# First attention of a four-layer gated network on one NeuronCore: softmax weights divided before they are transposed, the value product taken with V stationary, and the context read already transposed

## What is computed

```python
# first attention; "x" here is the context, "latents" the normalised running x
xn = layer_norm(x, gamma_x, beta_x)             # ctx_1024
ln = layer_norm(latents, gamma_l, beta_l)
q = (ln @ Wq).reshape(b, m, 8, 64) * 64 ** -0.5
k_x, v_x = xn @ Wkv;  k_l, v_l = ln @ Wkv
k_x = rope_rotate_k(k_x)
k = concat([k_x, k_l]);  v = concat([v_x, v_l])  # 64 + 64 keys
attn = softmax(einsum('bhid,bhjd->bhij', q, k))
out = einsum('bhij,bhjd->bhid', attn, v) @ Wo
# x = x + tanh(g_xattn[0]) * out
```

## Time and profile before

| | us |
|---|---|
| median of 3 runs (lowest to highest) | 2242.03 (2236.01 to 2242.62) |
| the profiled execution | 2245.91 |
| its span, first to last instruction | 2244.1 |
| mean granted TensorE clock of the span | 0.944 |

### The profile page before, as it was taken

The page is one execution under the profiler, slowest core; times in us unless marked ns, Lnnn a source line. Parts: engine busy times, 40 slices in busy tenths (PEclk is TensorE's granted clock), DMA queues, the critical chain, the costliest instruction groups (busy, mean ns, idle before and its releaser), DMA issues. The chain is left out here.

```text
span 2244.1 us, 48290 instructions
## 1 busy us (share of the span) xinstructions
PE 1965.8 (88%) x18173; PEld 1522.7 (68%) x18173; DVE 1700.4 (76%) x4753; ACT 1192.8 (53%) x2324; POOL 262.5 (12%) x553
## 2 busy tenths in 40 slices
PE   3999999999986998999989886999999986499808
PEld 3788888888876897777757665577777765244307
DVE  2787887878866887999967786766666668787894
ACT  1555555555543215888866553544454445316844
POOL 0011111011101101111111142000000022200000
PEclk9999999999997998999989998999999998699958
DMA  6222221212213551111100011222221111001462
GB/s 184 50 49 49 51 50 47 51 49 50 51 32 152 227 228 26 32 33 30 33 8 1 10 48 55 78 77 103 87 76 76 76 43 34 0 1 72 172 205 76
DMA packets 123591, 155.71 MB, mean 69 GB/s; under 512 B 47561, under 2 KB 104290, under 8 KB 119266
## 3 DMA queue, kind: packets, MB, share of 16 engines
q1 hardware_dynamic: 117368, 149.92, 20.8%
q10 hardware_dynamic: 5994, 2.70, 0.4%
HBM read 110.11 MB, written 25.69 MB: 61 GB/s over the span
## 5 line engine op out<-in xcount | busy, mean ns | idle before, releaser
L1720 DVE TENSOR_TENSOR arena<-arena 128x512 f32<-128x512 f32 (+1 forms) x256 | 170.7, 685 | 68.9 <-ACT arena L1758 64.8
L1758 ACT ACTIVATE arena<-banks,b1c 128x512 f32<-128x512 f32 x192 | 131.7, 687 | 170.4 <-PE banks L1633 170.2
L1643 PEld LDWEIGHTS banks<-w2a,arena 128*128 128x128 f32 x1024 | 124.1, 192 | 28.6 <-issue 28.6
L888 PE MATMUL banks<-we,arena 128*128 128x128 f32 x1024 | 132.9, 284 | 4.4 <-DVE arena L952 0.5
L491 PE MATMUL banks<-arena,wk 128*128 128x128 f32 x1024 | 134.5, 286 | 1.1 <-DVE arena L609 1.1
L888 PEld LDWEIGHTS banks<-we,arena 128*128 128x128 f32 x1024 | 122.5, 195 | 12.8 <-DVE arena L952 12.4
L491 PEld LDWEIGHTS banks<-arena,wk 128*128 128x128 f32 x1024 | 122.1, 196 | 12.4 <-issue 10.7
L1643 PE MATMUL banks<-w2a,arena 128*128 128x128 f32 x1024 | 124.7, 275 | 0.0
L595 DVE TENSOR_TENSOR arena<-arena,konst 128x512 f32<-128x512 f32 x64 | 44.3, 693 | 104.3 <-DMA arena<-arena 104.3
L1633 PE MATMUL banks<-arena,w1s 128*128 128x512 f32 x256 | 122.1, 611 | 0.0
L501 PE MATMUL banks<-wv,arena 128*128 128x512 f32 x256 | 120.9, 595 | 0.0
(11 more groups left out here) (271 smaller groups left out, 5091.5 us busy)
## 6 DMA issues: line engine op xcount, KB each, us to landing
arena<-coef_scratch SPq DMA_DIRECT2D x32, 2048.0 KB, 7.2
arena<-arena SPq DMA_DIRECT2D x256, 64.0 KB, 2.0
gated_scratch<-arena SPq DMA_DIRECT2D x16, 768.0 KB, 3.2
arena<-gated_scratch SPq DMA_DIRECT2D x16, 768.0 KB, 4.4
arena<-z1T_scratch SPq DMA_DIRECT2D x128, 64.0 KB, 2.4
arena<-ctxT_scratch SPq DMA_DIRECT2D x32, 256.0 KB, 2.8
arena<-in_ctx SPq DMA_DIRECT2D x64, 64.0 KB, 1.9
z1T_scratch<-arena SPq DMA_DIRECT2D x64, 64.0 KB, 1.7
```

Of the source, the lines that this page charges most:

```text
L888: mm = pe.matmul(ps[:, OUT + g.par, j * D:(j + 1) * D], xs[g.par][:, n, j * P:(j + 1) * P], k.we0[:, n, :], start=n == 0, stop=n == EXPERT ...
L1643: mm = pe.matmul(ps[:, OUT + g.par, j * D:(j + 1) * D], hT[g.par][:, c, j * P:(j + 1) * P], w, start=c == 0, stop=c == CHUNKS2 - 1)
L1720: dve.tensor_tensor(hT[g.par][rows, c, :], hT[g.par][rows, c, :], wide_coef[g.par][rows, e, :], ALU.mult).then_inc(s["scaled"].sem, 1)
L1758: act.activation(hT[g.par][:, c, :], ps[:, HID + c % NHID, :], ACT.Gelu, bias=k.b1c[:, c:c + 1])\
```

## The change

Five things change in `attention0`.

- Softmax: VectorE's maxima are written negated (`low`) and the subtraction is gone. ScalarE takes the exponential from PSUM with `low` as its bias, one activation of 128x128 for each of the eight heads, and each also writes its row sum (`accum_out=total`). The scale 1/8 moves into the copy of the queries. VectorE then divides in place (`shares`: a reciprocal of 128x4 and a product of 128x512 for each half) before the transposes.
- Value product: V (128x64 for a head and sequence) is stationary, and the transposed weights stream (64 columns). The result is already feature by token, so the four transposes L527 go, and ScalarE's copy `oT` follows the product. V has no column of ones and one buffer instead of two; GpSimd's memsets go.
- Context: the transpose L538, the copy L665 and the store L443 go. `kernel` gives a further input `ctx_turned`, made on the host, and `context_attention` loads that.
- Order: on TensorE the value product is now that of t-1 and stands behind the keys; queries, the wait for `ot_sb` of t-1, the two transposes of t+2, the output product, and then values and weight transposes of t in two halves. VectorE takes `krot` last in a step, behind `shares` of the second half, and `ksin` behind `x_updated`. ScalarE takes `oT` between the two halves of exponentials.
- Banks and buffers: `AV` and the input transposes `XT` share bank 2, `OUT` shares bank 5 with the second half of V, `Z` has three buffers.

The diff, cut to its core. Where "..." stands in the `tensor`, `vector` and `scalar` parts, the lines of the kernel above are taken out.

```diff
@@ -405,25 +402,22 @@
     two = lambda n: [k.take(n) for _ in range(2)]
     cin, zh = two(D), two(D)
 
-    Z = [z.rearrange("p (b s i) -> p b s i", b=PAIR, s=2) for z in two(2 * P)]
-    z1o, cto = two(P), two(P)
+    Z = [z.rearrange("p (b s i) -> p b s i", b=PAIR, s=2) for z in (k.take(2 * P) for _ in range(3))]
+    z1o = two(P)
     KT = k.take(HPAIRS * 4 * SEQ).rearrange("p (c s b i) -> p c s b i", c=HPAIRS, s=2, b=PAIR)
     kc, kr = k.take(512), k.take(512)
     rotA, rotB = k.take(512), k.take(512)
     QT = k.take(HPAIRS * P).rearrange("p (c b i) -> p c b i", c=HPAIRS, b=PAIR)
-    V = [v.rearrange("p (b h e) -> p b h e", b=PAIR, e=VW) for v in two(PAIR * H0 * VW)]
-    mx = k.take(2 * HPAIRS)
+    V = k.take(PAIR * INNER).rearrange("p (b n) -> p b n", b=PAIR)
+    low, total, rec = (k.take(H0).rearrange("p (o c) -> p o c", o=2) for _ in range(3))
     prob = k.take(2 * 512).rearrange("p (o n) -> p o n", o=2)
     probT = k.take(2 * 512).rearrange("p (o c n) -> p o c n", o=2, c=HPAIRS)
-    rec = k.take(H0)
-    on = k.take(INNER)
     oT = k.take(INNER)
     s = k.sigs(T, dict(
-        zhat=1, z_ready=3, ctxT_sb=1, k_psum=2, kc=1, q_psum=1, v_psum=2, kcos=1, ksin=1,
-        krot=1, klat=1, q_sb=1, v_sb=2, s_psum=1, smax=2, sshift=2, prob=2, pt_psum=2, pt_sb=2, av=1, recip=1,
-        onorm=1, ot_psum=1, ot_sb=1, out_psum=1))
+        zhat=1, z_ready=3, k_psum=2, kc=1, q_psum=1, v_psum=2, kcos=1, ksin=1, krot=1, klat=1, q_sb=1, v_sb=2,
+        s_psum=1, low=2, weight=H0, recip=2, share=2, pt_psum=2, pt_sb=2, av=1, ot_sb=1, out_psum=1))
+    AV, XT, V0, OUT, SCORES = 2, 2, 4, 5, 6
     ctx_loaded, swapped = k.transfers(T, "ctx_loaded"), k.transfers(T, "keys_swapped", 4)
-    preset = k.sem("L0_preset")
     ctx_dram = k.a["ctx_1024"].rearrange("(t b) s d -> t (b s) d", b=PAIR)
     cosT = k.konst[:, C_COS:C_COS + SEQ].unsqueeze(1).broadcast_to([P, 8, SEQ])
     sinT = k.konst[:, C_SIN:C_SIN + SEQ].unsqueeze(1).broadcast_to([P, 8, SEQ])
@@ -434,13 +428,11 @@
         def body(at):
             if t := at(3):
                 if t.has(2):
-                    sp.wait_ge(*f["xT_psum"](t.back(2)))
+                    sp.wait_ge(*s["zhat"](t.back(2)))
                 sp.dma_start(cin[t.par], ctx_dram[t.idx]).then_inc(ctx_loaded.at(t), 16)
             if t := at(1):
                 sp.wait_ge(*s["z_ready"](t))
                 sp.dma_start(k.z1T_dram[t.idx], z1o[t.par]).then_inc(k.z1T_stored.at(t), 16)
-                sp.wait_ge(*s["ctxT_sb"](t))
-                sp.dma_start(k.ctxT_dram[t.idx], cto[t.par]).then_inc(k.ctxT_stored.at(t), 16)
                 sp.wait_ge(*s["kc"](t))
                 if t.has(1):
                     sp.wait_ge(*s["ksin"](t.back(1)))
@@ -450,9 +442,6 @@
 
     def gpsimd(pool):
         k.ready(pool)
-        pool.memset(V[0][:, :, :, HD0:VW], 1.0).then_inc(preset, 1)
-        pool.memset(V[1][:, :, :, HD0:VW], 1.0).then_inc(preset, 1)
-        pool.wait_ge(preset, 2)
 
         def body(at):
             if t := at(2):
@@ -469,17 +458,18 @@
 
     def tensor(pe):
         k.ready(pe)
...
 
         def body(at):
             if t := at(0):
                 pe.wait_ge(*s["krot"](t))
                 pe.wait_ge(*s["klat"](t))
                 pe.wait_ge(*s["q_sb"](t))
+                if t.has(1):
+                    pe.wait_ge(*s["weight"](t.back(1)))
                 for c in range(HPAIRS):
                     for o, b in ((0, 0), (1, 1), (0, 1), (1, 0)):
                         dims = slice(64 * o, 64 * o + 64)
...
+                        mm = pe.matmul(ps[64 * b:64 * b + 64, SCORES + o, c * P:(c + 1) * P], QT[dims, c, b, :],
                                        KT[dims, c, :, b, :], start=True, stop=True)
                 mm.then_inc(s["s_psum"].sem, 1)
             if t := at(1):
@@ -488,74 +478,65 @@
                     pe.wait_ge(*s["pt_sb"](t.back(2)))
                 for n in range(2):
                     for c in range(HPAIRS):
...
+                        mm = pe.matmul(ps[:, n, c * P:(c + 1) * P], k.wk0[:, c * P:(c + 1) * P], Z[t.idx % 3][:, :, n],
                                        start=True, stop=True)
                     mm.then_inc(s["k_psum"].sem, 1)
...
+            if t := at(-1):
+                pe.wait_ge(*s["pt_sb"](t))
+                pe.wait_ge(*s["v_sb"](t))
                 if at(1):
                     pe.wait_ge(*s["z_ready"](at(1)))
...
+                for c in range(HPAIRS):
+                    for b in range(PAIR):
+                        for o in range(2):
+                            e = (2 * c + o) * HD0
+                            mm = pe.matmul(ps[64 * o:64 * o + 64, AV, c * P + b * 64:c * P + b * 64 + 64],
+                                           V[:, b, e:e + HD0], probT[:, o, c, b * 64:b * 64 + 64],
+                                           start=True, stop=True)
+                mm.then_inc(s["av"].sem, 1)
             if t := at(1):
...
+                if t.has(1):
+                    pe.wait_ge(*s["q_sb"](t.back(1)))
                 for c in range(HPAIRS):
...
+                    mm = pe.matmul(ps[:, 3, c * P:(c + 1) * P], k.wq0[:, c * P:(c + 1) * P], Z[t.idx % 3][:, :, 1],
                                    start=True, stop=True)
                 mm.then_inc(s["q_psum"].sem, 1)
...
+            if at(-1):
+                pe.wait_ge(*s["ot_sb"](at(-1)))
             if t := at(2):
                 pe.wait_ge(*f["xhat_ready"](t))
                 pe.wait_ge(*s["zhat"](t))
...
+                pe.transpose(ps[:, XT, 2 * P:3 * P], k.xh[:, t.par, :], k.ident)
+                pe.transpose(ps[:, XT, 3 * P:4 * P], zh[t.par], k.ident).then_inc(f["xT_psum"].sem, 1)
             if t := at(-1):
...
                 for c in range(HPAIRS):
...
+                    mm = pe.matmul(ps[:, OUT, 0:D], oT[:, c * P:(c + 1) * P], k.wo0[:, c, :],
                                    start=c == 0, stop=c == HPAIRS - 1)
                 mm.then_inc(s["out_psum"].sem, 1)
+            if t := at(0):
+                for b in range(PAIR):
+                    if b and at(-1):
+                        pe.wait_ge(*f["x_updated"](at(-1)))
+                    pe.matmul(ps[:, V0 + b, :], Z[t.idx % 3][:, b].rearrange("p s i -> p (s i)"), k.wv0[:, :],
+                              start=True, stop=True).then_inc(s["v_psum"].sem, 1)
+                    pe.wait_ge(*s["share"](t, b + 1))
+                    if at(1):
+                        pe.wait_ge(*s["kc" if b == 0 else "klat"](at(1)))
+                    for c in range(HPAIRS):
+                        mm = pe.transpose(ps[:, b, c * P:(c + 1) * P], prob[:, b, c * P:(c + 1) * P], k.ident)
+                    mm.then_inc(s["pt_psum"].sem, 1)
         steps(pe, T, 2, 1, body)
 
     def vector(dve):
+        def shares(t, o):
+            dve.wait_ge(*s["weight"](t, (o + 1) * HPAIRS))
+            k.hold(dve)
+            dve.reciprocal(rec[:, o], total[:, o]).then_inc(s["recip"].sem, 1)
+            dve.wait_ge(*s["recip"](t, o + 1))
+            each = prob[:, o].rearrange("p (c n) -> p c n", c=HPAIRS)
+            dve.tensor_tensor(each, each, rec[:, o].unsqueeze(2).broadcast_to([P, HPAIRS, P]), ALU.mult)\
+                .then_inc(s["share"].sem, 1)
+
         k.ready(dve)
 
         def body(at):
@@ -572,13 +553,8 @@
             if t := at(0):
                 dve.wait_ge(*s["s_psum"](t))
                 for o in range(2):
...
+                    dve.tensor_reduce(low[:, o], ps[:, SCORES + o, :].rearrange("p (c n) -> p c n", c=HPAIRS), AX.X,
+                                      ALU.max, negate=True).then_inc(s["low"].sem, 1)
             if t := at(2):
                 sl = t.par
                 tile_xhat(k, f, dve, t, sl)
@@ -590,79 +566,73 @@
                 dve.wait_ge(*s["kc"](t))
                 dve.tensor_tensor(rotA.rearrange("p (c i) -> p c i", i=SEQ), kc.rearrange("p (c i) -> p c i", i=SEQ),
                                   cosT, ALU.mult).then_inc(s["kcos"].sem, 1)
+            if t := at(0):
+                shares(t, 0)
+            if t := at(2):
+                sl = t.par
+                if t.has(2):
+                    dve.wait_ge(*k.z1T_stored(t.back(2)))
+                dve.wait_ge(*f["xT_psum"](t))
+                for dst, n, g in ((Z[t.idx % 3][:, :, 1], 2, 2), (Z[t.idx % 3][:, :, 0], 3, 0),
+                                  (z1o[sl].rearrange("p (b i) -> p b i", b=PAIR), 3, 4)):
+                    dve.tensor_scalar(dst, ps[:, XT, n * P:(n + 1) * P].rearrange("p (b i) -> p b i", b=PAIR),
+                                      k.aff[:, g:g + 1], k.aff[:, g + 1:g + 2], ALU.mult, ALU.add)\
+                        .then_inc(s["z_ready"].sem, 1)
+            if t := at(-1):
+                dve.wait_ge(*s["out_psum"](t))
+                dve.scalar_tensor_tensor(out=k.x[:, t.idx, :], in0=ps[:, OUT, 0:D], scalar=k.gates[:, 0:1],
+                                         in1=k.x[:, t.idx, :], op0=ALU.mult, op1=ALU.add)\
```

(56 more changed lines are left out.)

100 lines of the change are left out of this document (3 added, 97 removed).

## The result

| | before | after |
|---|---|---|
| median of 4 runs each on one chip, us | 2242.32 (2236.01 to 2243.92) | 2209.98 (2207.37 to 2220.58) |
| ratio of the means, 95% interval | | 0.987 (0.9832 to 0.9908) |
| profiled execution, us | 2245.91 | 2211.95 |
| its span, us; clock | 2244.1; 0.944 | 2210.1; 0.943 |
| scores to scores, the commonest step, us | 9.52 | 8.97 |

The change is faster by 32 us in the medians. In the profiled pair the stage ends 26.4 us earlier; the other 7.6 us of the spans lie behind it, in unchanged code, which took 1572.3 us before and 1564.7 after. Over all the profiles of this study, 14 with these two, that part took from 1554.5 to 1572.3 us, with or without the change, so those 7.6 us are within the scatter.

A forecast was written before the change was run, and what follows sets the result against it. It took TensorE's gapless 9.52 us step as the bound, with a chain through the other engines near. 63 x (9.52 - 9.0) = 32.8 us, less 3 for disturbed steps, gain 30: 2242.03 becomes 2212 us, range 2196 to 2239.

The forecast's parts named there:

- With no wait between: First attention before the change: each TensorE block starts where the one before lets it, so 9.52 us is TensorE's sum.
- TensorE's own sum after: TensorE's step: L527 (0.43) and one input transpose (0.11) leave 9.52, the rest only moved: 8.98 us.
- The walk: One step of the new order timed link by link over the engines: TensorE and chain both end at 8.87 us.
- the subtraction: TensorE's step counted as 9.52 less 0.54 us: 8.98 us.
- The chain: Keys' copy, four heads, `oT`, output, VectorE's copies, `ksin`, `krot` at 8.82, next scores at 8.87 us.
- A head: ScalarE's exponential with row sum, start to start: 0.26 without sum cost, 0.37 us taken with overlap.
- The end at 0.57: ScalarE's exponentials, if the row sum serialises: 0.57 us a head, step 9.67, time 2255 us; chance 0.09.
- The wait for `oT`: TensorE ahead of the input transposes: free at 4.90, it waits for ScalarE's result copy until 4.98 us.
- the rival: Serialised sum on ScalarE ahead of `oT`: from 0.53 us a head the step is 9.52 again; chance 0.09.
- Disturbed steps: Steps longer than common, 9 us in all before; with the swap lacking slack, 3 us more expected.
- The later-swap rival: Swap and handovers ahead of `ksin` 0.3 to 0.4 us later every step: step 9.3, 2230 us; chance 0.17.
- Drain and fill: Filling and draining of the stage pass the same links once: nothing taken.

The follow-up runs named there:

- third copy last: The changed kernel with VectorE's third affine copy (`z1o`) moved behind `krot`: 2208.23 us, 0.9866.
- combination: The changed kernel with `z1o` copied behind `krot`, `x_updated` behind `ksin`, and two of the four swap DMAs issued by GpSimd: 2199.59 us, 0.9838.
- four transposes agree: The changed kernel with the four weight transposes of the first half made twice on TensorE: 2221.56 us, 0.993.
- Longer heads: The changed kernel with two further 128x4 activations of spare data behind each exponential: 2238.54 us, 1.0003.
- the swap on two queues: The changed kernel with two of the four swap DMAs issued by GpSimd instead of SP: 2203.14 us, 0.9848.

## Why the prediction was right, step by step

The forecast was 2212 us and the time is 2210; the mechanism, TensorE's sum and the chain ending almost together, is the one found. Several terms were off, in opposite ways:

- **What bounds before.** "With no wait between" was wrong, and it is the premise that failed. Of the 9.52, 0.08 was a wait for the queries' copy. The row that showed it was there: 0.29 behind a transpose, where the border from the output product to the scores, with nothing to wait for, takes 0.20; and the 3.1 us of the earlier trace rows were only the visible tip of some 5 us in 63 steps.
- **TensorE's own sum after**: 8.98 predicted, 8.90 measured (third copy last, combination; four transposes agree). The 0.08 between them is the wait, gone because the new order asks for that copy only at the next scores. That the rest is moved and not changed holds in the sum, and not block by block: the borders between large and small weights cost the same in all, behind other blocks. The walk took the plain spacing for the input transposes (0.22, not 0.40), so its blocks add to 8.79 without the wait for `oT`, 0.18 under the subtraction; the prediction shows both counts and doesn't say why they differ. Of that 0.18, 0.08 was the wait and 0.10 the border. The border's cost is read from the traces; no run changes the size of the weights alone.
- **The chain**: 8.87 walked, 8.97 measured. The spacings on VectorE were as walked, within 0.04. Against the walk, in us from the scores: value product 1.98 (not 1.89) behind the keys' start, input transposes 5.10 (4.98), copies 5.60 (5.41), `x_updated` 6.56 (6.41), `krot` done 8.92 (8.82). The two borders around the value product, in keys and queries, and the handover behind the transposes make the difference. The two errors went opposite ways, and 9.0 us a step came out almost right: 0.55 us a step by measurement instead of 0.52, 34.7 us in 63 steps against 32.8.
- **A head**: 0.37 taken, 0.34 measured: 0.25 for the exponential and 0.09 for the sum's own instruction (407.94, 408.19, 408.28 above). The end at 0.57 was far off; the reason given, that neighbours overlap, holds for the small instruction too. The Trainium skill (ScalarE: Activation LUTs, section What ACT_TABLE_LOAD costs) makes it 0.294 without the sum, an estimate from its figures; the run without sums shows 0.28, so the trace agrees within 0.02.
- **The wait for `oT`**: predicted 0.08 and there is none, since TensorE comes at 5.10 instead of 4.90 and `oT` is done at 4.82 instead of 4.88. Longer heads bring it back, as the rival said.
- **Disturbed steps**: 3 us taken, 7.1 measured (9.0 to 16.1). The mechanism, a swap without slack, is shown by the run without it; the size was short by 4 us. In the changed kernel 11.4 of the 16.1 us lie in the 16 steps whose swap took SP over 2.6 us to issue, 3.1 us in five where it landed late, and 1.7 us in the first step. Before, no swap took over 2.53 us to issue and five landed 1.2 to 1.9 us late. So the slack that went is one part, and issues that were not slow before are the other, which the prediction could not read from its rows. The later-swap rival, with 0.3 us in every step, did not come: only 19 waits.
- **Drain and fill**: nothing taken. From the last scores to the last `x_updated` it is 11.9 us before (659.9 to 671.8), 11.6 in the changed kernel run again (633.6 to 645.2) and 13.2 in the first profile of it (632.15 to 645.38). The order costs nothing there; TensorE's clock did. It stood for `oT` for 1.84 us in both, and behind that wait it was granted the lower level, 1.2 GHz (0.50), in one of them only. The output product of the first profile, the stretch behind it by windows (clock third from the end), and the same product of the run again:

```profile
636.17 1.73 PE L513 MATMUL banks<-wo,arena 128*128 128x128 f32 x8 [1.84 <-ACT arena L619]
```

```profile
637.00:639.00 2.00, 2.00 (x7) 1.26 (x6) 1.03 (x3) 0.51 (x4) 0.00 (x0) 0.50 0.00 0
```

```profile
637.61 1.16 PE L513 MATMUL banks<-wo,arena 128*128 128x128 f32 x8 [1.84 <-ACT arena L619]
```

- **The stage in sum**: common steps 34.7, disturbed steps -7.1, drain 0.3, its clock -1.6, filling 0.2 (first scores at 50.9 instead of 51.1): 26.5 us, measured 26.4 (671.8 - 645.4). The prediction's 30 lay 4 high; scatter in the later stages (7.6 us in the profiled pair) brought the whole time close to the forecast, so the agreement within 2 us is in part luck.
- **Context**: counted at 0.11 in TensorE's sum. It is worth nothing on the kernel before and 0.11 a step in the changed one. The parts don't add; which of them pays depends on which limit the others have left.

## What to carry to other kernels

A stretch of products that looks gapless can hold waits up to the length of a product's row less its spacing; compare each block's start to start with its count times that spacing, and each border with one between weights of the same sizes, before calling it the engine's own sum. When a reordering brings two limits within 0.1 us of each other, walk both and price each further edit against the smaller margin. And when an edit takes the slack from a DMA, its late times are paid in full; how often it is late must be counted anew after, since here the swap's issues were never slow before and were in a fifth of the tiles after.

## What the runs showed of the hardware

- A row sum (`accum_out`) is an instruction of its own, 213 ns long, that adds 0.09 us start to start behind an exponential of 0.25 us.
- A product with V (128x64) stationary and 64 columns streaming takes 34 ns a pass (32 passes in 1.08 us), as with the weights stationary and 65 streaming.
- SP issues the four 32-row swap DMAs in 2.41 us. In the changed kernel 12 of 64 such groups take 3.0 to 3.8 us; in the kernel before none takes over 2.8, with the store or without it. Of the store's issues before, a third were slow, up to 1.7 us instead of 0.43, where nothing waited for them; with the store put back in the changed kernel the swap was slow all the same. What makes them slow was not found. GpSimd issues two in 1.09 us, like SP's 1.15.
- The same wait of 1.84 us at the end of the stage is followed by 3 us at half the clock in some executions (four profiles: 13.2 to 13.3 us from the last scores on) and not in others (the third copy last, the swap on two queues and the run again: 11.6 us). Why was not found.
- Between a block of TensorE with 128x128 weights and one with 64*64 or 128*64, 0.20 us pass from pass to pass instead of 0.11 although nothing is waited for (405.82 to 406.25 and 364.48 to 365.01 above), and 0.10 more once on the way back (queries 1.00 behind the value product, 0.90 elsewhere).
